# A four-layer graph network on one core: the last linear map of layers 0 and 3 per node, VectorE in place of TensorE for one masking step, and more picked columns

## The reference, cut to what matters

```python
h = relu(layernorm(x))                                  # ahead of each of the four layers
# layer 0 (32 edge features, hidden width 128)
x = x + segment_sum(relu([h[dst], h[src], ea32] @ W1 + b1) @ W2 + b2, dst)
# layer 1: softmax over the edges of a destination, then ELU
x = x + elu(segment_sum(h[src] * softmax_by_dst(edge_weight)[:, None], dst))
# layer 2: the maximum over the edges of a destination
x = x + segment_max((h[dst] - h[src]) @ theta.T + theta_b + (h @ phi.T + phi_b)[src], dst)
# layer 3 (16 edge features, hidden width 128)
m = relu(relu([h[src], h[dst], ea16] @ W1 + b1) @ W2 + b2) @ W3 + b3
x = h + segment_sum(m, dst) / max(count, 1)
```

## Time and profile before

| | us |
|---|---|
| median of 3 runs (7792.11 to 7808.14) | 7793.15 |
| the profiled execution, its own time | 7796.36 |
| its span | 7794.6 |
| PE busy / DVE busy / ACT busy / POOL busy | 6659.6 / 5210.7 / 2085.6 / 5823.6 |
| mean granted TensorE clock | 0.941 |

### The profile page before, as it was taken

The page is one execution under the profiler, slowest core; times in us unless marked ns, Lnnn a source line. Parts: engine busy times, 40 slices in busy tenths (PEclk is TensorE's granted clock), DMA queues, the critical chain, the costliest instruction groups (busy, mean ns, idle before and its releaser), DMA issues.

```text
span 7794.6 us, 87563 instructions
## 1 busy us (share of the span) xinstructions
PE 6659.6 (85%) x29454; PEld 5473.0 (70%) x29454; DVE 5210.7 (67%) x6271; ACT 2085.6 (27%) x5004; POOL 5823.6 (75%) x6117
## 2 busy tenths in 40 slices
PE   0799999999669999999479999999139999999992
PEld 0688888888557777777367777777127777777771
DVE  6577777777667777777767777777545666666663
ACT  5133333333212222222300000000014444444441
POOL 7777777777777777777767777777777777777776
PEclk9999999999879999999689999999569999999995
DMA  8354544444323333333223333333124444444441
GB/s 321 84 113 112 113 111 113 112 112 113 84 62 83 82 82 88 82 82 82 59 63 74 74 74 77 75 74 74 44 59 98 100 98 98 98 98 99 98 99 42
DMA packets 1063994, 722.05 MB, mean 93 GB/s; under 512 B 583026, under 2 KB 970916, under 8 KB 1063428
## 3 DMA queue, kind: packets, MB, share of 16 engines
q1 hardware_dynamic: 850448, 510.81, 23.7%
q0 software_dynamic: 197008, 163.26, 13.7%
q10 hardware_dynamic: 16100, 42.39, 1.4%
HBM read 478.38 MB, written 237.49 MB: 92 GB/s over the span
## 4 chain that ended last, share of the span: by engine, by line
POOL 48%; issue 16%; PE 6%; DVE 3%; DMA 1%; ACT 0%; POOLq 0%; DVEq 0%
POOL G L683 42%; POOL R L702 5%; PE pOdd L905 4%; PE pRows L905 1%; POOL first_rows L644 1%; DVE onehot L1288 1%; DVE S L1337 1%; PE pRows L1002 0%; PE pOdd L897 0%; DVE G L1300 0%; ACT G L828 0%; DMA G<-table,e_dst 0%; DMA G<-table,idx 0%; DVE pT L1322 0%; DMA prefix<-O 0%
## 5 line engine op out<-in xcount | busy, mean ns | idle before, releaser
L683 POOL DMA_INDIRECT G<-table,idx x2923 | 2758.3, 944 | 891.0 <-issue 878.2
L683 POOL DMA_INDIRECT G<-table,e_dst x2497 | 2362.8, 946 | 790.7 <-issue 753.7
L1223 DVE TENSOR_TENSOR_SCAN K<-mask_f,K,pT 48x512 f32<-48x512 bf16 x782 | 1005.4, 1286 | 1242.5 <-PE pT L970 1117.0
L1002 PEld LDWEIGHTS pRows<-w,S 128*128 128x128 f32 x6256 | 1573.9, 324 | 304.4 <-issue 179.2
L905 PE MATMUL pOdd<-h_high,onehot 128*128 128x480 f32 (+1 forms) x3880 | 1519.5, 392 | 0.0
L905 PE MATMUL pOdd<-h_low,onehot 128*128 128x480 f32 (+1 forms) x3880 | 1489.6, 384 | 0.0
L1002 PE MATMUL pRows<-w,S 128*128 128x48 f32 x6256 | 1445.3, 374 | 2.1 <-ACT O L838 0.5
L905 PE MATMUL pRows<-h_high,onehot 128*128 128x480 f32 (+1 forms) x2430 | 952.6, 392 | 85.1 <-DVE h_low L1076 85.1
L905 PE MATMUL pRows<-h_low,onehot 128*128 128x480 f32 (+1 forms) x2430 | 920.4, 379 | 0.0
L1288 DVE TENSOR_TENSOR onehot<-mask_f,pEven 128x2560 fp32r<-128x2560 f32 (+1 forms) x390 | 892.1, 2288 | 19.4 <-DMA mask_f<-pick_row 19.4
L905 PEld LDWEIGHTS pOdd<-h_high,onehot 128*128 128x128 f32 x3880 | 749.8, 193 | 128.5 <-issue 3.9
(11 more groups left out here) (203 smaller groups left out, 8666.6 us busy)
## 6 DMA issues: line engine op xcount, KB each, us to landing
mask_f<-same_row SPq DMA_DIRECT2D x392, 256.0 KB, 3.3
prefix<-O SPq DMA_DIRECT2D x194, 512.0 KB, 3.6
G<-first_rows SPq DMA_DIRECT2D x784, 96.0 KB
prefix<-O SPq DMA_DIRECT2D x390, 192.0 KB
G<-table,idx POOLq DMA_INDIRECT x2923
G<-table,e_dst POOLq DMA_INDIRECT x2497
first_rows<-zeros ACTq DMA_DIRECT2D x14, 2688.0 KB, 15.5
K<-in_ea_dram SPq DMA_DIRECT2D x588, 64.0 KB
```

The lines of the kernel that those rows point to most:

```text
L683: pool.indirect_dma_start(rows[:, slot, j, 0:widths[l]], None, table[l], bass.IndirectOffsetOnAxis(ap=at[:, n, j:j + 1], axis=0))\
L1002: last = pe.matmul(o, s[:, :, j], (w2_0 if l == 0 else w3_3)[:, :], start=True, stop=True)
L1223: dve.tensor_tensor_scan(K[r, c.slot, :], mask_of(c, r), pT[c.slot % 2][r, :], K[r, (c.slot - 1) % RING, CHUNK - 1:CHUNK], ALU.mult, ALU.add)\
```

## The change

It has four parts.

1. In layers 0 and 3, `make_rows` becomes `turn_rows`: PE only transposes the 128-wide hidden sums of a chunk, SP stores rows of 128 instead of 48, and the product with W2 (layer 0) or W3 (layer 3) is made once per node block, after POOL has fetched the node's last sum: seven PE transposes, two ACT copies and seven matmuls per round q, ahead of DVE's work on that round.
2. The masking matmul `hide_unchosen` on PE is gone. DVE instead overwrites the wrong spans in PSUM: one scalar_tensor_tensor (minus 3e38 times the flag, plus the sum), in place, ahead of each maximum, with a wait on its end between the two.
3. Picks. Layer 0: every second chunk instead of every third (190 columns for 126, beside the same 16 early ones). Layers 1 and 2: seven chunks of eight (342 and 339 for 317 and 314). Layer 3: every third chunk instead of every sixth (126 for 63). The lag between marking and placing a pick in layer 0 goes from 5 to 4, in layer 3 from 6 to 5.
4. In layer 3 the hidden scan comes one step later (stage lag 3 for 2), as do the second matmul and the rows; W1's product has one bank instead of two. The ring of stored rows has 4 places instead of 8.

```diff
-PICK_SLOTS = (1, 2, 3, 5, 6, 7)
+PICK_SLOTS = (1, 2, 3, 4, 5, 6, 7)
-EDGE_PICK_CYCLE = {0: 3, 3: 6}
-EDGE_PICK_LAG = {0: 5, 3: 6}
+EDGE_PICK_CYCLE = {0: 2, 3: 3}
+EDGE_PICK_LAG = {0: 4, 3: 5}
...
-    row_width = [D, WIDE, WIDE, D]
+    row_width = [HID, WIDE, WIDE, HID]
...
-            def hide_unchosen(out, i):
-                pe.matmul(out[:, 0:SPAN * D], minus_big[:, :],
-                          unchosen[:, i, :].rearrange("p (s o) -> p s o", o=1).to_broadcast([P, SPAN, D]),
-                          start=True, stop=False)
...
+            def multiply_rows(v, q):
+                before_q, s = 2 * (TURNED_BEFORE[v] + q), q % 2
+                pe.wait_ge(last_rows_in[v][s], (q // 2 + 1) * 16 * NODE_BLOCKS)
+                if q:
+                    pe.wait_ge(hidden_copied, before_q)
+                for i, (first, stop) in enumerate(TURN_BANKS):
+                    for k in range(first, stop):
+                        last = pe.transpose(pT[i][:, (k - first) * P:(k - first + 1) * P], R_hidden[:, s, k, :], ident[:, :])
+                    last.then_inc(hidden_turned, 1)
+                if q:
+                    pe.wait_ge(last_rows_used[v], q)
+                for i, (first, stop) in enumerate(TURN_BANKS):
+                    pe.wait_ge(hidden_copied, before_q + i + 1)
+                    for k in range(first, stop):
+                        last = pe.matmul(node_rows[:, k, :], R_turned[:, s, k, :], (w2_0 if v == 1 else w3_3)[:, :],
+                                         start=True, stop=True)
+                last.then_inc(nodes_multiplied, 1)
...
-                        o = rows_bank[l][c.n % len(rows_bank[l])][:, j * w:(j + 1) * w]
-                        last = pe.matmul(o, s[:, :, j], (w2_0 if l == 0 else w3_3)[:, :], start=True, stop=True)
+                        o = rows_bank[l][c.n % len(rows_bank[l])][:, j * HID:(j + 1) * HID]
+                        last = pe.transpose(o, s[:, :, j], ident[:, :])
...
-                stages = {0: [(0, transpose_rows), (1, layer_1), (3, make_rows), (0, sum_edge_pick)],
-                          3: [(0, transpose_rows), (1, layer_1), (3, make_rows), (1, layer_2), (0, sum_edge_pick)]}[l]
+                stages = {0: [(0, transpose_rows), (1, layer_1), (3, turn_rows), (0, sum_edge_pick)],
+                          3: [(0, transpose_rows), (1, layer_1), (4, turn_rows), (2, layer_2), (0, sum_edge_pick)]}[l]
...
+                    link(dve.scalar_tensor_tensor(sums, unchosen[:, flags, :].rearrange("p (b o) -> p b o", o=1)
+                                                  .to_broadcast([P, SPAN, D]), -BIG, sums, ALU.mult, ALU.add))
                     dve.tensor_reduce(G[:, slot, j, 0:D],
                                       out[:, 0:SPAN * D].rearrange("p (b d) -> p d b", d=D), AX, ALU.max)
...
-                          3: [(0, spread_dst), (0, place_edge_pick), (0, mark_edge_pick), (2, scan)]}[l]
+                          3: [(0, spread_dst), (0, place_edge_pick), (0, mark_edge_pick), (3, scan)]}[l]
```

More of the change, by code:

```diff
@@ L60, in stream_picks @@
 def stream_picks(chunks):
-    return [n for n in range(chunks) if n % RING in PICK_SLOTS or n % (2 * RING) == PICK_EXTRA]
+    return [n for n in range(chunks) if n % RING in PICK_SLOTS]
 def edge_picks(l, chunks):
@@ L802, in relu_1 @@
                     act.wait_ge(hidden1[l], c.n + 1)
-                    bank = pH1[c.slot % 2]
+                    bank = first_bank[l][c.n % len(first_bank[l])]
                     if l == 0:
@@ L906, in add_group @@
                                      part[:, first:stop, :].rearrange("p b d -> p (b d)"),
-                                     start=False, stop=g == PICK_GROUPS - 1 and part is h_low)
+                                     start=g == 0 and part is h_high, stop=g == PICK_GROUPS - 1 and part is h_low)
                 return last
-            def hide_unchosen_of(d):
-                for k, i in enumerate(picks_of(d)):
-                    hide_unchosen(pick_sum[d % 2][:, k, :], i)
             def add_rows(d, g):
@@ L941, in sum_picks, with sum_first_picks @@
                     last.then_inc(picks_summed[l], 1)
+            def multiply_rows(v, q):
[9 more added lines that the diff above has]
+                    pe.wait_ge(last_rows_used[v], q)
+                for i, (first, stop) in enumerate(TURN_BANKS):
+                    pe.wait_ge(hidden_copied, before_q + i + 1)
[3 more added lines that the diff above has]
+                last.then_inc(nodes_multiplied, 1)
+            def sum_first_picks(blocks):
+                for g in range(PICK_GROUPS):
+                    if -(-min((g + 1) * SPAN, B) // NODE_BLOCKS) != blocks:
+                        continue
+                    if g == 0:
+                        pe.wait_ge(picks_marked[1], 2)
+                    pe.wait_ge(split_made, SPLIT_BEFORE[1] + blocks)
+                    for d in range(2):
+                        last = add_rows(d, g)
+                    if g == PICK_GROUPS - 1:
+                        last.then_inc(picks_summed[1], 2)
             for l in range(4):
```

123 lines of the change are left out of this document (73 added, 50 removed).

## The result

The changed kernel takes 7999.58 us (median of 4 runs, 7997.12 to 8002.58) where the kernel before takes 7792.63: a ratio of 1.026, 95% interval 1.024 to 1.028. The forecast was 7923, with a range up to 7990. The sign was right. The loss of 207 us is more than half as large again as the 130 that the sum held, and the time lies 10 us above the range.

What follows compares the result with a forecast made beforehand. POOL was taken as the bound, giving way to loops through DVE and PE in layers 0, 1 and 2. 173+18-78.5+7+10 = +129.5 on 7796.4 gave 7925.9, forecast as 7923 us after 3.2 for the median; range 7765 to 7990.

Steps and rivals of the forecast that it cites:

- the price of the transposes in layer 0: Layer 0, PE: four transposes of a chunk's hidden sums were taken to cost 0.83 us, with 0.44 as a rival.
- the clock survives an idle time of 2.3 us: Layers 1 and 2: PE idles 2.3 us per cycle behind the one-pick sum, with the clock still near 0.98.
- POOL as the bound: All layers: POOL starts one gather per 1.247 us; 177 fewer gathers would save at most 221 us.
- The added pass on DVE: DVE's overwriting before each maximum: 0.66 us plus 0.03 for the wait, 0.69; 1.19 for two picks.
- The loop of layer 0: Layer 0: a closed loop through DVE and PE takes 10.06 us per two chunks, above POOL's 8.73; +173 us.
- since the loads stay what they were: Layer 0, PE: strided loads keep their 0.2075 us each when products become transposes, so four take 0.83.
- The cycle of layers 1 and 2: Eight chunks take 32.17 us through the chain over DVE, against POOL's 31.16; +9 us in each layer.
- The row at 2.44 is against it: Argument against the clock rival: after one PE idle time of 2.44 us matmuls did not slow to 0.40 us apart.
- the clock: Rival, layers 1 and 2: 98 stalls each drop PE's clock to 1.2 GHz, costing 225 us: 8148; 8%.
- Cheap transposes: Rival, layer 0: strided operands cost nothing in transposes, the loop is 9.67, 74 us shorter: 7849; 21%.
- Layer 3: POOL stays the bound at 13.71 us per three chunks; 63 fewer gathers give -78.5, with +3 and +4 against it.
- Node phases and set-up: Node phases after layers 0 and 3: +10 us for both; set-up: some 3 us more on DVE, beside POOL's scatters.

Runs made afterwards that it cites:

- e4: The changed kernel with marks ahead of the scan in layers 1 and 2, and lag 5 instead of 4 in layer 0: 7583.95 us, 0.973 of the kernel before.
- e1: The changed kernel with nine matmuls of constants on PE behind every single-pick sum in layers 1 and 2: 7867.03 us.

## Why the prediction was wrong

Two steps failed: the price of the transposes in layer 0, and the reading that the clock survives an idle time of 2.3 us in layers 1 and 2. The rest held.

*POOL as the bound, and 221 us as the ceiling*: right; e4 comes within 12 us of it.

*The added pass on DVE*: right, 0.663 us where I took 0.66, and 1.16 where I took 1.16. A pass over the same bank with the same columns was the row to go by. The slope in the prediction, 1.1 to 1.5 ns per column, should read 1.2 to 1.5 (1160/960 and 514/336); nothing hangs on it.

*The loop of layer 0*: right in its parts, place and releaser. PE waits before W1's product for the scan L1305, 297 us in total; the row of the waits is

```profile
PE pEven L1016 <- DVE S L1305: 296.7, 194, 2.3
```

Mis-sized in one term, the transposes: 0.39 for 0.83, 83 us too much. The step that failed is "since the loads stay what they were": the 0.2075 was measured on products, and the form of the instruction changed with the edit. The nearer row was that of the transposes of a chunk, 0.11 each, close to the 0.39 for four. I had it, as the rival. The 0.15 us from the scan to PE stands in no row of before; it measured 0.16 (1219.89 to 1220.05 above). For the twenty matmuls of a pick the prediction has 4.42 in one sum and 4.24 in another, where its own price of 2.17 for ten gives 4.34; both are PE's own work, which set the pace in neither layer.

*The cycle of layers 1 and 2*: 32.17 forecast, 32.40 where the clock stays. Right as far as it goes. The step that failed is "The row at 2.44 is against it", the reading of the earlier trace rows: one idle time of 2.44 us that the clock survived. From it I held 2.3 to be safe and gave the clock 8%. One row isn't a bound where the same idle time recurs 98 times. In the new trace 2.16 us are survived in 4 of 46 cases. And the trace of the kernel before already held the contrary, in layer 2, of which the earlier trace rows shows nothing: five idle times of PE between 2.2 and 2.4 us (2.24, 2.26, 2.28, 2.36 and 2.38), and behind all five the matmuls start 0.40 us apart. One of them, and then the window behind it, whose granted clock is 0.50:

```profile
4288.78 0.58 PE L897 MATMUL pOdd<-unchosen,minus_big 128*128 128x480 fp8e4 x2 [2.28 <-DVE onehot L1288]
...
4289.93 0.60 PE L905 MATMUL pOdd<-h_high,onehot 128*128 128x480 f32 x1
4290.33 0.60 PE L905 MATMUL pOdd<-h_low,onehot 128*128 128x480 f32 x1
```

```profile
4289.30:4292.70 3.40, 3.40 (x10) 2.79 (x9) 3.40 (x7) 0.00 (x0) 2.67 (x3) 0.50 0.12 22
```

What tells the survived idle times from the others the runs don't show. PE makes no transposes in layers 1 and 2, so what the prediction says of transposes and the clock had nothing to act on there. The errors of the two terms have opposite signs, +166 and -82, so by luck the total looks better than its parts.

*The range*: it took the rivals one at a time. Cheap transposes and the clock both came true. With the prices that the prediction gave them that is 7849+225 = 8074, 74 us too much; only with the measured 1.6 us for each of some 90 falls is it 7849+144 = 7993, within 7 us of the measured time. Rivals that concern different layers don't exclude each other, and I should have added them; the range would then have held the time.

*Layer 3*: right, -84 for -71.5; the cheaper transposes also shorten its drain, which I only infer from the table.

*Node phases and set-up*: +3 and +2 for +10; the start is 5.7 later where I took nothing, since POOL's scatters themselves end that much later (302.08 and 307.80). Why they do I didn't try.

## What to carry to other kernels

When an edit moves work from one engine to another, follow the ring around it, not the busy shares: which instruction releases the next, through both engines, and back. The order within a step on the slower side (marks ahead of a scan, or marks and placing in different steps) was worth 250 and 172 us here, with no instruction added or taken away; what each of the four parts of the change is worth alone was not measured, except the masking in layers 1 and 2. And an idle time of TensorE costs more than its length once the clock falls behind it; a few matmuls of constants in the gap were then cheaper than the gap (133 us less in e1).

## What I had not expected of the hardware

The granted clock fell after 42 of 46 idle times of 2.16 us and 1.6 us were lost each time; it never fell in the cycles with 1.27, 0.88 or 0.74. In the kernel before it fell after 2.24 to 2.38 in layer 2 and stayed after 2.44 in layer 1, so the length of the idle time alone doesn't decide. A stationary operand of 128x128 in fp32 that takes every fourth element costs 0.105 us more per instruction in a product (1.66 against 0.82 for eight) and 0.009 more in a transpose (0.39 against 0.355 for four).
